# A decoder layer on one core: TensorE's order in the first row tile of a group of heads, with the packed halves apart, the reciprocals earlier and the values product in two halves

## The chip, the cores and the metric

The kernel runs on one core of a Trainium2 chip. The metric is the device time of the whole program in microseconds (us), the median of several runs; lower is better. Matrix products, transposes and weight loads run on TensorE (PE, weight loads shown as PEld), elementwise work on VectorE (DVE), exponentials and copies on ScalarE (ACT), small elementwise work on GpSimd (POOL); DMAs are issued from SyncE (SP). Each engine works through its own instructions in the order in which they are written, and the engines wait for one another only through semaphores.

## What is computed

One layer of a decoder: causal-by-multiplication attention with 16 heads, a second attention in which the layer's own rows are mixed by a softmax over a context, and a gated feed-forward part whose weights are packed in four bits.

```python
def reference(x, ctx_1024, Wq, Wk, Wv, Wo, xWq, xbq, xWk, xbk, gate_p, gate_s, up_p, up_s, down_p, down_s):
    # x: (4, 512, 512), 16 heads of 32
    x = x + attn(layernorm(x));  x = x + xattn(layernorm(x), ctx_1024);  return x + ffn(layernorm(x))

def attn(x):
    q, k, v = (x @ Wq), (x @ Wk), (x @ Wv)             # each reshaped to (B, T, 16, 32)
    scores = einsum('bthd,bshd->bhts', q, k) * tril(ones((T, T)))
    out = einsum('bhts,bshd->bthd', softmax(scores / T ** 0.5), v)
    return out.reshape(B, T, 512) @ Wo
```

The mask multiplies the scores: beyond the diagonal a score is 0, not minus infinity, so those columns still carry a weight, exp(0 - max), in the sum and in the product with the values.

## The kernel before

**Tiling.** The four batches (n = 0 to 3) go one after the other. A batch's attention is cut into 16 units (`UNITS`): four groups of four heads (`HG`), and in each group four row tiles of 128 rows (`TT`), u = 4 * group + row tile. Row tile i looks at (i + 1) * 128 columns (`wide`), so the first row tile of a group (u = 0, 4, 8, 12) is the narrowest and the fourth the widest. What lies beyond is one sum of values (`v_beyond`), scaled by one exponential (`e_zero`).

**The steps of one head j of one unit u**, each on its engine:

- `scores` (L929, PE) multiplies queries and keys of head j into bank j, once the exponentials of that head one unit back have read it;
- `row_max` (L1600, DVE) scales, masks and takes the largest of each row; `shift` (L763, POOL) negates it;
- `exp` (L1257, ACT) writes the weights `prob`;
- `turn` (L940, PE) transposes them, one 128x128 block at a time, into one of the banks 4, 5 and 7;
- `turned` (L1273 on ACT for heads 0 to 2, or 0 and 1 in a fourth row tile; L1610 on DVE for the rest) copies the transposed weights out, `prob_t`.

And once per unit: `recips` (L970, PE) turns the four columns of reciprocals into one bank of the same three, `recip_out` (L1279, ACT) copies it out; `values` (L961, PE) multiplies the transposed weights with V, four heads beside one another in columns of 32 (a 128x32 tile of the array), and `divide` (L1638, DVE) scales the product. Per 128 columns `values` has four matmuls, one per head, and for row tiles 0 to 2 four more for what lies beyond. All of them are float32, and a float32 matmul into a 128x32 tile is two records in the trace.

**Repacking.** Once per group a piece of the packed feed-forward weights is transposed as well: `repack` (L1036, PE) writes twelve 16-bit transposes, six into each of two banks; the first half is cast out by ACT (`pk_t`, L1293), the second by DVE (L1651), and SP stores both.

**The three shared banks.** Turns, reciprocals and the two packed halves go through banks 4, 5 and 7 in turn. A step's place in that sequence is its slot; `turn_slot`, `recip_slot` and `pack_slot` give it, and the bank is slot modulo three. Before PE writes slot s it waits (`turn_read`) until slot s - 3 has been read, by whichever engine reads that one.

**The order on PE** is written out by hand in `body` (L1201 on). In unit u, for each head j: the scores of unit u + 1, then the turn of unit u. After head 3 come the reciprocals and the values of unit u - 1. In the first row tile of a group (u = 4, 8, 12) both packed halves of the group before stand behind head 1. ACT's, DVE's and POOL's orders are written out in the same way; ACT's place for the cast of the first packed half is behind the copy of the turned head 1 (L1500).

In the text below, S(u,j) is a scores instruction, T(u,j) a turn, R(u) the reciprocals and V(u) the values of unit u.

Of the kernel before, what the change touches and what calls it, by code (L numbers as in the profile page):

```python
# [36 lines left out]
F16 = mybir.dt.float16  # L37
# [9 lines left out]
P = 128  # L47
# [5 lines left out]
TT = T // P  # L53
KT = D // P
HG = HEADS // 4
UNITS = HG * TT
# [35 lines left out]
def decoder_layer(nc, x, ctx_1024, Wq, Wk, Wv, Wo, xWq, xbq, xWk, xbk, gate_p, gate_s, up_p, up_s, down_p, down_s, out):  # L92
    with ExitStack() as ctx:
        def sem(name):
            return ctx.enter_context(nc.semaphore(name))
# [28 lines left out]
        def sb(name, shape, dt):  # L124
            return first.enter_context(nc.sbuf_tensor(name, shape, dt))
# [20 lines left out]
        pk_16 = sb("pk_16", [P, 6, C], F16)  # L146
# [9 lines left out]
        ident16 = sb("ident16", [P, P], F16)  # L156
# [98 lines left out]
        pt_act, pt_dve, av_done, o_done, o_hi, o_lo = (sem(n) for n in ("pt_act", "pt_dve", "av_done", "o_done", "o_hi", "o_lo"))  # L255
# [5 lines left out]
        pk_conv, pk_full, pk_out0, pk_out1, pk_stored = (sem(n) for n in ("pk_conv", "pk_full", "pk_out0", "pk_out1", "pk_stored"))  # L261
# [14 lines left out]
        ROWS = 4 * UNITS  # L276
        wide = [(i + 1) * P for i in range(TT)]

        def turn_slot(h):


            return h + 2 * (max(0, h - 2) // 16) + max(0, h // 4 - 1)

        def copied_by_act(u):

            return 2 if u % TT == TT - 1 and u < UNITS - 1 else 3

        def act_copies(n, u):

            return sum(copied_by_act(v) for v in range(UNITS)) * n + sum(copied_by_act(v) for v in range(u + 1))  # L290

        def vector_copies(n, u):

            return 4 * (n * UNITS + u + 1) - act_copies(n, u)

        def pack_slot(r, half):
            return (turn_slot(16 * r + 17) + 1 if r < HG - 1 else recip_slot(UNITS - 2) + 1) + half

        def recip_slot(u):
            return turn_slot(4 * u + 7) + 1 if u < UNITS - 1 else pack_slot(HG - 1, 1) + 1  # L300

        def turn_bank(slot):
            return bank[(4, 5, 7)[slot % 3]]

        def turn_read(n, slot):

            for u in range(UNITS):
                if slot == recip_slot(u):
                    return rden_out, n * UNITS + u + 1
                for j in range(4):  # L310
                    if slot == turn_slot(4 * u + j):
                        mine = copied_by_act(u)
                        return (pt_act, act_copies(n, u) - mine + j + 1) if j < mine else (pt_dve, vector_copies(n, u) - 3 + j)
            r, half = next((r, half) for r in range(HG) for half in range(2) if slot == pack_slot(r, half))
            return (pk_out0, pk_out1)[half], n * (NB // B) + r + 1
# [10 lines left out]
        def beyond_units(n, u):  # L326

            return n * HG * (TT - 1) + u // TT * (TT - 1) + min(u % TT + 1, TT - 1)
# [544 lines left out]
        def _(pe):  # L873
# [58 lines left out]
            def turn(n, u, j):  # L932
                i, slot = u % TT, turn_slot(4 * u + j)
                pe.wait_ge(exp_done, n * ROWS + 4 * u + j + 1)
                if slot < 3:
                    pe.wait_ge(att_lo, n * KT + (2, 3, 4)[slot])
                if slot >= 3:
                    pe.wait_ge(*turn_read(n, slot - 3))
                for k in range(wide[i] // P):
                    mm = pe.transpose(turn_bank(slot)[:, P * k:P * k + P], prob[:, u % 2, j, P * k:P * k + P], ident[:])  # L940
                mm.then_inc(t_full, 1)

            def values(n, u):

                hg, i = u // TT, u % TT
                pe.wait_ge(pt_act, act_copies(n, u))
                pe.wait_ge(pt_dve, vector_copies(n, u))
                if u == 0:
                    pe.wait_ge(v_out, n * TT + TT)
                if u >= 1:  # L950
                    pe.wait_ge(o_done, n * UNITS + u)
                blocks = wide[i] // P
                at = P * (u % 2)
                if i < TT - 1:
                    pe.wait_ge(v_zero_done, beyond_units(n, u))
                for k in range(blocks + (i < TT - 1)):
                    for j in range(4):
                        h = 4 * hg + j
                        lhs, rhs = (V[:, k, DH * h:DH * h + DH], prob_t[:, u % 2, j, P * k:P * k + P]) if k < blocks else \
                                   (v_zero[:, u % 2, DH * j:DH * j + DH], ident[:])  # L960
                        mm = pe.matmul(bank[6][32 * j:32 * j + 32, at:at + P], lhs, rhs, start=(k == 0), stop=(k == blocks - (i == TT - 1)))  # L961
                mm.then_inc(av_done, 1)

            def recips(n, u):

# [56 lines left out]
                        mm = pe.transpose(bank[CONTEXT_BANK[k]][:, P * m:P * m + P], e_p[:, m, P * k:P * k + P], ident[:])  # L1022
                    mm.then_inc(att_full, 1)

            def repack(n, r):
                nb = n * (NB // B) + r
                pe.wait_ge(pk_conv, 6 * nb + 6)
                for half in range(2):
                    pe.wait_ge(*turn_read(n, pack_slot(r, half) - 3))
                    bk = turn_bank(pack_slot(r, half))[:].bitcast(F16)  # L1030

                    tiles = [[(0, 0), (1, 0)], [(0, 1), (1, 1)], [(2, 0), (3, 0)]] if half == 0 else \
                            [[(2, 1), (3, 1)], [(4, 0), (4, 1)], [(5, 0), (5, 1)]]
                    for q in range(3):
                        for e, (a, w) in enumerate(tiles[q]):
                            mm = pe.transpose(bk[:, 256 * q + P * e:256 * q + P * e + P], pk_16[:, a, P * w:P * w + P], ident16[:])  # L1036
                    mm.then_inc(pk_full, 1)

            def product(m, x, which, pair, slot, nb):

# [160 lines left out]
            def body(n, last):  # L1201
                for u in range(UNITS):
                    for j in range(4):
                        if u + 1 < UNITS:
                            scores(n, u + 1, j)
                        turn(n, u, j)
                        if j == 3 and u == UNITS - 1 and not last:
                            pe.wait_ge(ln_done[0], (n + 2) * TT)
                            spread(0, n + 1, 0)
                        if j == 1 and u == UNITS - 1:  # L1210
                            values(n, u - 1)
                        if j == 3 and u > 0:
                            recips(n, u - 1)
                            if u < UNITS - 1:
                                values(n, u - 1)
                        if j == 1 and u % TT == 0 and u > 0:
                            repack(n, u // TT - 1)
                repack(n, HG - 1)
                recips(n, UNITS - 1)
                values(n, UNITS - 1)  # L1220
                between(n, True, not last)

            walk(body)(pe)


# [814 lines left out]
```

## Time and profile before

| | |
|---|---|
| median of 3 runs | 1477.64 us (1476.62 to 1477.94) |
| the profiled execution | 1479.39 us, of which its span 1477.7 us |
| busy share of the span | PE 96%, DVE 67%, ACT 48%, POOL 26% |
| granted TensorE clock | 1.00 |
| attention stages | about 70 to 135, 201 to 264, 333 to 396 and 467 to 528 us |
| one group of heads inside them | 15.13 us |

The page gives busy time per engine over the span, in 40 slices; the attention stages are those in which PE falls to 8 or 9 tenths while ACT rises. The timeline lists instructions in order of start; in it the number in brackets is the idle time of that engine ahead of the instruction, with what ended it.

### The profile page before, as it was taken

What the parts mean: (1) busy time and instruction counts of PE and PEld (TensorE: products, weight loads), DVE (VectorE), ACT (ScalarE), POOL (GpSimd) and SP (SyncE); (2) the same over time, 40 slices, a digit from 0 to 9 for tenths busy, and PEclk for the clock granted to TensorE, in tenths of its full rate; (3) what the DMA queues carried; (4) which work ended last, traced back from release to release, by engine and by line L of the source; (5) the groups of instructions that cost most, each with busy time, mean ns of one, the idle gap of its engine ahead of it and who ended that gap; (6) DMA issues with size and microseconds to landing.
All of it is one profiled execution on the core that took longest, in us unless ns stands there. A gap on an engine that the chain in (4) does not pass through costs nothing.

```text
span 1477.7 us, 26838 instructions
## 1 busy us (share of the span) xinstructions
PE 1422.8 (96%) x8896; PEld 718.8 (49%) x8896; DVE 990.5 (67%) x2125; ACT 716.6 (48%) x1660; POOL 380.5 (26%) x691
## 2 busy tenths in 40 slices
PE   6989998998998999999999999999999999999999
PEld 3465456556645654344444444444444444444444
DVE  7786688678668767886566666665665766665533
ACT  5795279239716845344354353353343443533532
POOL 0053225304373436521221112112112212212100
PEclk9999999999999999999999999999999999999999
DMA  7554622352456521000000001001001001000011
GB/s 249 143 159 125 171 70 83 113 161 66 142 160 171 180 63 45 17 24 25 31 14 22 17 17 33 17 17 35 17 17 32 17 16 33 17 17 1 0 58 57
DMA packets 76877, 98.01 MB, mean 66 GB/s; under 512 B 8000, under 2 KB 60736, under 8 KB 76224
## 3 DMA queue, kind: packets, MB, share of 16 engines
q1 hardware_dynamic: 76736, 96.23, 21.5%
q8 instruction: 76, 1.25, 0.4%
q14 instruction: 65, 0.53, 0.1%
HBM read 68.94 MB, written 27.26 MB: 65 GB/s over the span
## 4 chain that ended last, share of the span: by engine, by line
PE 84%; issue 5%; ACT 5%; DVE 4%; POOL 1%; DMA 0%; ACTq 0%; POOLq 0%; DVEq 0%; SPq 0%
PE bank L876 25%; PE bank L877 24%; PE bank L878 24%; ACT prob L1257 3%; PE bank L940 3%; PE bank L961 2%; PE bank L929 1%; PE bank L889 1%; PE bank L1001 1%; PE bank L1016 1%; PE bank L970 1%; PE bank L1011 1%; ACT prob_t L1273 1%; DVE xt L1585 1%; PE bank L1022 1%
## 5 line engine op out<-in xcount | busy, mean ns | idle before, releaser
L876 PE MATMUL bank<-xs,G 128*128 128x512 f16 x896 | 339.8, 379 | 2.5 <-issue 1.4
L877 PE MATMUL bank<-xs,G 128*128 128x512 f16 x896 | 339.6, 379 | 0.0
L878 PE MATMUL bank<-xs,G 128*128 128x512 f16 x896 | 339.6, 379 | 0.0
L1345 ACT COPY c<-bank 128x512 f32<-128x512 f32 x192 | 111.4, 580 | 220.2 <-PE bank L878 215.4
L1730 DVE TENSOR_TENSOR c<-bank,c 128x512 f32<-128x512 f32 x128 | 88.1, 689 | 193.7 <-PE bank L878 193.7
L876 PE MATMUL bank<-Wd,hid 128*128 128x512 f16 x512 | 194.1, 379 | 2.8 <-DVE X L1784 2.8
L878 PE MATMUL bank<-Wd,hid 128*128 128x512 f16 x512 | 194.0, 379 | 0.0
L877 PE MATMUL bank<-Wd,hid 128*128 128x512 f16 x512 | 194.0, 379 | 0.0
L748 POOL TENSOR_TENSOR c<-c,m 128x512 f32<-128x512 f32 x64 | 82.4, 1287 | 389.2 <-ACT c L1345 389.2
L1784 DVE SCALAR_TENSOR_TENSOR X<-bank,col,X 128x512 f32<-128x512 f32 x128 | 95.4, 750 | 101.5 <-PE bank L878 101.3
L1600 DVE CUSTOM_DVE_ANT_0 bank<-bank,mask,col 128x128 f32<-128x128 f32 (+3 forms) x256 | 139.3, 549 | 25.8 <-issue 17.2
L1257 ACT ACTIVATE prob<-bank,nmx 128x128 f32<-128x128 f32 (+3 forms) x256 | 146.6, 581 | 0.7
L876 PEld LDWEIGHTS bank<-xs,G 128*128 128x128 f16 x896 | 87.7, 98 | 114.2 <-ACT c L1345 6.1
L878 PEld LDWEIGHTS bank<-xs,G 128*128 128x128 f16 x896 | 87.7, 98 | 105.7
L877 PEld LDWEIGHTS bank<-xs,G 128*128 128x128 f16 x896 | 87.7, 98 | 103.1
L940 PE MATMUL bank<-ident,prob 128*128 128x128 f32 x640 | 111.9, 277 | 13.0 <-ACT prob L1257 3.8
L1368 ACT CAST hid<-c 128x512 f16<-128x512 f32 x128 | 79.2, 619 | 90.4 <-DVE c L1744 87.2
L1360 ACT ACTIVATE c<-c,col 128x512 f32<-128x512 f32 x96 | 69.4, 723 | 94.1 <-DVE c L1730 94.1
L763 POOL TENSOR_TENSOR nmx<-zero,mx 128x1 f32<-128x1 f32 x256 | 51.2, 200 | 236.1 <-DVE mx L1600 207.4
L1750 DVE TENSOR_TENSOR hid<-c,hid 128x512 f16<-128x512 f32 x128 | 86.1, 713 | 25.7 <-ACT hid L1368 25.7
L705 POOL TENSOR_TENSOR w_sum<-w_full 128x384 f32<-128x384 f32 (+1 forms) x30 | 22.1, 737 | 314.2 <-DVE w_full L1711 314.1
L940 PEld LDWEIGHTS bank<-ident,prob 128*128 128x128 f32 x640 | 76.0, 140 | 30.8 <-issue 19.3
(192 smaller groups left out, 2406.0 us busy)
## 6 DMA issues: line engine op xcount, KB each, us to landing
stack<-qk_dram SPq DMA_DIRECT2D x128, 128.0 KB, 3.3
sc_in<-scale_t SPq DMA_DIRECT2D x30, 384.0 KB
qk_dram<-qk SPq DMA_DIRECT2D x32, 256.0 KB, 2.8
packed_t<-pk_t SPq DMA_DIRECT2D x32, 192.0 KB, 2.0
pk_in<-packed_t SPq DMA_DIRECT2D x30, 192.0 KB
X<-in_x_dram SPq DMA_DIRECT2D x4, 1024.0 KB, 6.2
pk_in<-L_ffn_gate_W_packed_dram SPq DMA_DIRECT2D x16, 256.0 KB, 2.7
pk_in<-n_L_ffn_up_W_packed_dram SPq DMA_DIRECT2D x16, 256.0 KB, 3.1
```

Of the source, the lines that this page charges most:

```text
L748: nc.gpsimd.tensor_tensor(c22[x][:], c22[x][:], m5[x][:], ALU.add).then_inc(c22_out, 1)
L876: pe.matmul(o, lhs(0), rhs(0), start=first, stop=False, skip_group_check=onto)
L877: pe.matmul(o, lhs(0), rhs(1), start=False, stop=False, skip_group_check=onto)
L878: return pe.matmul(o, lhs(1), rhs(0), start=False, stop=stop, skip_group_check=onto)
L940: mm = pe.transpose(turn_bank(slot)[:, P * k:P * k + P], prob[:, u % 2, j, P * k:P * k + P], ident[:])
L1257: nc.scalar.activation(prob[:, u % 2, j, 0:wide[i]], bank[j][:, 0:wide[i]], ACT.Exp, bias=nmx[:, u % 2, j:j + 1], accum_out=den[:, u % 2, ...
L1345: nc.scalar.copy(dst[:], bank[BANK_Y if which == M5 else x][:]).then_inc(c_copied, 1)
L1368: nc.scalar.copy(hid[:, beta, q, r, 0, :], quarter(1, idx)[:]).then_inc(hid_hi, 1)
L1600: nc.vector.tensor_tensor_reduce(out=bank[j][:, 0:wide[i]], in0=bank[j][:, 0:wide[i]], in1=mask[:, P * (3 - i):P * (3 - i) + wide[i]], sca ...
L1730: nc.vector.tensor_tensor(dst[:], bank[at][:], dst[:], ALU.add).then_inc(comb, 1)
L1750: nc.vector.tensor_tensor(hid[:, beta, q, r, 1, :], quarter(1, idx)[:], hid[:, beta, q, r, 0, :], ALU.subtract).then_inc(hid_lo, 1)
L1784: nc.vector.scalar_tensor_tensor(xv, bank[4 + t][:], C_OUT, xv, ALU.mult, ALU.add).then_inc(acc_out, 1)
```

## The change

Only the order on PE in units 4, 8 and 12 of each batch is different, twelve places in all, and the slots with it. ACT, DVE, POOL and SP execute the same instructions in the same order as before; only the bank numbers of some of their copies are others.

- The first packed half goes behind head 0's turn, the second behind head 1's, instead of both behind head 1's.
- The reciprocals of unit u - 1 go behind the second packed half, instead of behind head 3.
- The values of unit u - 1 (always a fourth row tile, 16 matmuls) are cut in two: eight behind head 2's turn, eight behind head 3's.

```diff
+        slots_in_turn = []
+        for u in range(UNITS):
+            for j in range(4):
+                slots_in_turn.append(("turn", 4 * u + j))
+                if u > 0 and u % TT == 0 and j < 2:
+                    slots_in_turn.append(("pack", u // TT - 1, j))
+                if u > 0 and j == (1 if u % TT == 0 else 3):
+                    slots_in_turn.append(("recip", u - 1))
+        slots_in_turn += [("pack", HG - 1, 0), ("pack", HG - 1, 1), ("recip", UNITS - 1)]
+
         def turn_slot(h):
-            return h + 2 * (max(0, h - 2) // 16) + max(0, h // 4 - 1)
+            return slots_in_turn.index(("turn", h))
...
         def pack_slot(r, half):
-            return (turn_slot(16 * r + 17) + 1 if r < HG - 1 else recip_slot(UNITS - 2) + 1) + half
+            return slots_in_turn.index(("pack", r, half))
         def recip_slot(u):
-            return turn_slot(4 * u + 7) + 1 if u < UNITS - 1 else pack_slot(HG - 1, 1) + 1
+            return slots_in_turn.index(("recip", u))
...
-            def values(n, u):
+            def values(n, u, parts=(0, 1)):
                 hg, i = u // TT, u % TT
+                total = wide[i] // P + (i < TT - 1)
+                ks = range(0 if 0 in parts else total // 2, total if 1 in parts else total // 2)
...
-                for k in range(blocks + (i < TT - 1)):
+                for k in ks:
...
-                mm.then_inc(av_done, 1)
+                if 1 in parts:
+                    mm.then_inc(av_done, 1)
...
-            def repack(n, r):
+            def repack(n, r, half):
...
-                        if j == 3 and u > 0:
+                        first_tile = u % TT == 0 and u > 0
+                        if first_tile and j < 2:
+                            repack(n, u // TT - 1, j)
+                        if u > 0 and j == (1 if first_tile else 3):
                             recips(n, u - 1)
-                            if u < UNITS - 1:
-                                values(n, u - 1)
-                        if j == 1 and u % TT == 0 and u > 0:
-                            repack(n, u // TT - 1)
-                repack(n, HG - 1)
+                        if first_tile and j > 1:
+                            values(n, u - 1, (j - 2,))
+                        if j == 3 and 0 < u < UNITS - 1 and not first_tile:
+                            values(n, u - 1)
+                repack(n, HG - 1, 0)
+                repack(n, HG - 1, 1)
                 recips(n, UNITS - 1)
                 values(n, UNITS - 1)
```

PE's order in unit 4 of the first batch, before, from the turn of head 0 to the first scores of unit 6 (`prob` is a turn, `stack` scores, `pk_16` a packed half, `r_col` the reciprocals, `prob_t,V` the values):

```order
L940 MATMUL bank5<-ident,prob 128x128
L929 MATMUL bank1<-stack 128x256
L940 MATMUL bank7<-ident,prob 128x128
L1036 MATMUL bank4<-ident16,pk_16 128x128 x6
L1036 MATMUL bank5<-ident16,pk_16 128x128 x6
L929 MATMUL bank2<-stack 128x256
L940 MATMUL bank7<-ident,prob 128x128
L929 MATMUL bank3<-stack 128x256
L940 MATMUL bank4<-ident,prob 128x128
L970 MATMUL bank5<-ident,r_col 32x128 x4
L961 MATMUL bank6<-prob_t,V 32x128 x16
L929 MATMUL bank0<-stack 128x384
```

The same stretch of PE's order in the changed kernel, from the first packed half on:

```order
L1047 MATMUL bank7<-ident16,pk_16 128x128 x6
L938 MATMUL bank1<-stack 128x256
L949 MATMUL bank4<-ident,prob 128x128
L1047 MATMUL bank5<-ident16,pk_16 128x128 x6
L982 MATMUL bank7<-ident,r_col 32x128 x4
L938 MATMUL bank2<-stack 128x256
L949 MATMUL bank4<-ident,prob 128x128
L972 MATMUL bank6<-prob_t,V 32x128 x8
L938 MATMUL bank3<-stack 128x256
L949 MATMUL bank5<-ident,prob 128x128
L972 MATMUL bank6<-prob_t,V 32x128 x8
L938 MATMUL bank0<-stack 128x384
```

The reciprocals now stand ahead of the scores and turns of heads 2 and 3 and go into bank 7, which the first packed half wrote; before, it was the turn of head 3 that followed the first packed half in its bank. With their waits, PE's rows of the reciprocals and of head 3's turn at this place, before:

```order
L940 MATMUL bank4<-ident,prob 128x128 [waits pk_out0,exp_done]
L970 MATMUL bank5<-ident,r_col 32x128 [waits rcol_done,pk_out1]
```

and in the changed kernel, in its order:

```order
L982 MATMUL bank7<-ident,r_col 32x128 [waits rcol_done,pk_out0]
L949 MATMUL bank5<-ident,prob 128x128 [waits pk_out1,exp_done]
```

The wait for `pk_out0`, ACT's cast of the first packed half, moved from the turn of head 3 to the reciprocals, and that for `pk_out1`, DVE's cast, the other way. ACT's order around that cast, the same before and after but for line and bank numbers:

```order
L1273 COPY prob_t<-bank5 128x128 [waits av_done,t_full]
L1257 ACTIVATE prob,den<-bank3,nmx 128x128 [waits t_full,shift_done]
L1266 ACTIVATE e_zero<-nmx 128x4 [waits shift_done,v_zero_done,den_done]
L1273 COPY prob_t<-bank7 128x128 [waits av_done,t_full]
L1293 CAST pk_t<-bank4 128x768 [waits sd_stored,pk_full]
L1257 ACTIVATE prob,den<-bank0,nmx 128x256 [waits t_full,shift_done]
L1273 COPY prob_t<-bank7 128x128 [waits av_done,t_full]
```

The cast stays behind the copy of T(4,1); nothing moved here.

## Rows read from the trace of the kernel before

**Rows 1.** The page: PE's granted clock, engines' busy time and PE's largest chain shares.

```profile
PE 1422.8 (96%) x8896; PEld 718.8 (49%) x8896; DVE 990.5 (67%) x2125; ACT 716.6 (48%) x1660; POOL 380.5 (26%) x691
...
PEclk9999999999999999999999999999999999999999
```

**Rows 2.** Windows, two whole groups of batch 1: us, busy per engine, clock, DMA share.

```profile
218.24:233.38 15.14, 13.61 (x209) 9.88 (x205) 12.84 (x51) 14.20 (x53) 7.51 (x26) 1.00 0.23 76
233.38:248.51 15.13, 13.61 (x208) 9.87 (x204) 12.55 (x50) 14.19 (x53) 7.31 (x26) 1.00 0.27 86
```

**Rows 3.** ACT's timeline, unit 8's place in batch 1: start, duration, line, idle before.

```profile
230.19 0.27 ACT L1273 COPY prob_t<-bank 128x128 f32<-128x128 f32 x1 [0.54 <-PE bank L940]
...
230.81 0.26 ACT L1273 COPY prob_t<-bank 128x128 f32<-128x128 f32 x1
230.95 0.82 ACT L1293 CAST pk_t<-bank 128x768 int16<-128x768 f16 x1
231.64 0.51 ACT L1257 ACTIVATE prob<-bank,nmx 128x256 f32<-128x256 f32 x1
...
232.10 0.29 ACT L1273 COPY prob_t<-bank 128x128 f32<-128x128 f32 x1
...
233.01 0.49 ACT L1257 ACTIVATE prob<-bank,nmx 128x256 f32<-128x256 f32 x1
...
233.97 0.37 ACT L1273 COPY prob_t<-bank 128x256 f32<-128x256 f32 x1 [0.38 <-PE bank L940]
```

**Rows 4.** PE's timeline at the same place, from T(8,0) to T(9,0).

```profile
229.77 0.28 PE L929 MATMUL bank<-stack 128*128 128x256 f16 x1
229.89 0.27 PE L940 MATMUL bank<-ident,prob 128*128 128x128 f32 x1
230.00 0.27 PE L929 MATMUL bank<-stack 128*128 128x256 f16 x1
230.10 0.27 PE L940 MATMUL bank<-ident,prob 128*128 128x128 f32 x1
230.21 0.83 PE L1036 MATMUL bank<-ident,pk 128*128 128x128 f16 x12
230.88 0.27 PE L929 MATMUL bank<-stack 128*128 128x256 f16 x1
231.22 0.30 PE L940 MATMUL bank<-ident,prob 128*128 128x128 f32 x1
231.35 0.27 PE L929 MATMUL bank<-stack 128*128 128x256 f16 x1
231.92 0.30 PE L940 MATMUL bank<-ident,prob 128*128 128x128 f32 x1 [0.29 <-ACT pk_t L1293]
232.15 0.42 PE L970 MATMUL bank<-ident,r_col 128*32 128x128 f32 x8
232.39 1.06 PE L961 MATMUL bank<-prob_t,V 128*32 128x128 f32 x32
233.38 0.34 PE L929 MATMUL bank<-stack 128*128 128x384 f16 x1
233.55 0.38 PE L940 MATMUL bank<-ident,prob 128*128 128x128 f32 x2
```

**Rows 5.** All waits of the span, longest first: waited for us, times, longest us.

```profile
PE bank L940 <- ACT pk_t L1293: 3.5, 12, 0.3
```

**Rows 6.** PE's timeline: sixteen value records, then scores; reciprocals, then a packed half.

```profile
235.59 0.40 PE L961 MATMUL bank<-prob_t,V 128*32 128x128 f32 x8
235.81 0.40 PE L961 MATMUL bank<-ident,v_zero 128*32 128x128 f32 x8
236.14 0.39 PE L929 MATMUL bank<-stack 128*128 128x512 f16 x1
...
261.25 0.43 PE L970 MATMUL bank<-ident,r_col 128*32 128x128 f32 x8
261.61 0.84 PE L1036 MATMUL bank<-ident,pk 128*128 128x128 f16 x12
```

**Rows 7.** DVE's timeline at the place: the row maximum behind the first scores of unit 10.

```profile
233.90 0.63 DVE L1600 CUSTOM_DVE_ANT_0 bank<-bank,mask,col 128x384 f32<-128x384 f32 x1 [0.71 <-issue]
```

**Rows 8.** PE's timeline: its longest idle in the second half's start.

```profile
560.64 0.39 PE L876 MATMUL bank<-att_t,o_t 128*128 128x512 f16 x1 [1.19 <-DVE o_t L1585]
```

**Rows 9.** Windows, a stretch that holds the wait of rows 8.

```profile
535.00:590.00 55.00, 53.45 (x263) 26.07 (x262) 40.29 (x87) 25.81 (x43) 26.50 (x22) 1.00 0.14 41
```

More of the change, by code:

```diff
@@ L953, in values @@
                 at = P * (u % 2)
-                if i < TT - 1:
+                if i < TT - 1 and 1 in parts:
                     pe.wait_ge(v_zero_done, beyond_units(n, u))
-                for k in range(blocks + (i < TT - 1)):
+                for k in ks:
                     for j in range(4):
@@ L1023, in context_out @@
                     mm.then_inc(att_full, 1)
-            def repack(n, r):
+            def repack(n, r, half):
                 nb = n * (NB // B) + r
                 pe.wait_ge(pk_conv, 6 * nb + 6)
[L1028 to L1037, printed above, removed]
+                pe.wait_ge(*turn_read(n, pack_slot(r, half) - 3))
+                bk = turn_bank(pack_slot(r, half))[:].bitcast(F16)
+                tiles = [[(0, 0), (1, 0)], [(0, 1), (1, 1)], [(2, 0), (3, 0)]] if half == 0 else \
+                        [[(2, 1), (3, 1)], [(4, 0), (4, 1)], [(5, 0), (5, 1)]]
+                for q in range(3):
+                    for e, (a, w) in enumerate(tiles[q]):
+                        mm = pe.transpose(bk[:, 256 * q + P * e:256 * q + P * e + P], pk_16[:, a, P * w:P * w + P], ident16[:])
+                mm.then_inc(pk_full, 1)
             def product(m, x, which, pair, slot, nb):
```

## The prediction, made before the changed kernel ran

> **What bounds the kernel now.** The page comes first: TensorE (PE) is busy nearly all the time at full granted clock, the other engines far less [rows 1]. That is an average over stages. The change touches only attention, so the next view is the windows of two whole groups of heads [rows 2]. There PE is busy 13.6 of 15.13 us, and ScalarE (ACT) 14.2. ACT is the fuller engine: 15.13 - 14.19 leaves it 0.94 us of idle time in a group. ACT's timeline shows where that is: 0.54 us ahead of the copy of T(8,0) at 230.19 and 0.38 us ahead of the copy of T(9,0) at 233.97 [rows 3], together 0.92 us, which is all of it. Both times ACT waits for a turn on PE. So everywhere else in a group ACT runs without a pause and sets the pace, and at the first row tile PE does. A group becomes shorter or longer by as much as these two turns come earlier or later, and a delay of T(9,0) isn't made good afterwards, because ACT has no pause left to give until the next such place.
>
> The first gap lies ahead of everything that the change moves: T(8,0) follows V(6), and both keep their places. The second one is the change's: T(9,0) stands behind T(8,3), R(7), V(7) and S(10,0). PE's timeline of the place [rows 4] is to be read as a chain. T(8,3) starts at 231.92, released by ACT's cast of the first packed half (230.95 + 0.82 = 231.77, and 0.15 us until PE is at work). From there PE runs without a pause: R(7) at 232.15, V(7) at 232.39, S(10,0) at 233.38, T(9,0) at 233.55, and ACT's copy starts 0.42 us later. The same wait for the cast stands 12 times in the list of waits, with the same 0.3 us [rows 5]: three places in each of four batches, all alike.
>
> **What the change does to that chain.** The cast itself can't come sooner. ACT does it right behind the copy of T(8,1), at 230.95, and reaches that copy at 230.81 after other work [rows 3]. In the new order T(8,1) stands behind the first packed half. The twelve packed transposes take 230.88 - 230.21 = 0.67 us, one half 0.335 us, so T(8,1) moves from 230.10 to 230.44. A turn's copy follows its start by 0.30 us (229.89 to 230.19), so it is ready at 230.74, still 0.07 us before ACT comes. The second half then waits for the copy of T(8,0) and ends at about 230.95; DVE's cast of it moves by some 0.05 us, which nothing waits for. So the cast on ACT still ends at 231.77.
>
> What waits for that cast is different. The reciprocals now take the bank of the first packed half. PE executes in order, so behind R(7) stand S(9,2), T(8,2), S(9,3) and T(8,3); the first three ran before 231.92 in the old order, beside the cast [rows 4]. PE idles from 230.95 to 231.92, and all of this comes after it.
>
> The pieces, each from a row:
> - R(7) and then a full-array instruction: 261.61 - 261.25 = 0.36 us [rows 6].
> - scores, then a turn: 229.89 - 229.77 = 0.12 us [rows 4].
> - a turn, then 128x32 work: 232.15 - 231.92 = 0.23 us [rows 4].
> - sixteen value records, then scores: 236.14 - 235.59 = 0.55 us [rows 6]. That is half of V(7), which has 32 records and takes 0.99 us in one piece (233.38 - 232.39).
>
> New chain from 231.92: R(7) 0.36, S(9,2) 0.12, T(8,2) 0.23, first half of V(7) 0.55, S(9,3) 0.12, T(8,3) 0.23, second half 0.55, sum 2.16 us. S(10,0) starts at 234.08. Before it started at 233.38, 1.46 us behind the wait. The place becomes 0.70 us longer.
>
> The 0.70 us have two sources. Three instructions at 0.11 to 0.12 us that used to run beside the cast now run behind it: 0.34 us. And PE changes more often between the full array and 128x32 tiles. A turn is followed by its neighbour after 0.11 us (230.10 to 230.21) but by 128x32 work after 0.23, and 32 value records at the 0.0275 us that eight of them take (235.81 - 235.59 = 0.22) make 0.88 of the 0.99 us. Each change costs about 0.12 us. Before there are two behind the wait, afterwards five: 3 x 0.12 = 0.36 us. The split as such isn't visible in the trace of before; bounded by rows, a change costs between nothing (if it hid beside the wait for a semaphore) and 0.13 us. I take 0.12, since all four kinds of neighbours in the rows show 0.11 to 0.13.
>
> The Trainium skill, "TensorEngine Tiling (Array Packing)", section "Key Properties", says that changing the tiling mode drains TensorE, and "TensorE: Matmul & The Clock Gate", section "Step-by-step: what each phase is for", puts a drain at about 128 cycles, by my estimate 0.05 us at 2.4 GHz. By that the place would be 0.34 + 3 x 0.05 = 0.5 us longer and the kernel 6 us; the rows show more than twice that per change, and the sum goes by them.
>
> **Does ACT hide some of it?** T(8,2) moves from 231.22 to 231.92 + 0.36 + 0.12 = 232.40, and its copy to 232.70 instead of 232.10 [rows 3]. The 1.49 us of ACT's work between that copy and the idle time (233.97 - 0.38 - 232.10) end at 234.19. T(9,0) starts at 234.08 + 0.17 = 234.25, and its copy at 234.67. So PE stays last, ACT idles 0.48 us in place of 0.38, and ACT's copy moves by the whole 0.70 us. ACT copies R(7) out ahead of the exponential that started at 233.01 [rows 3], so even 0.6 us later its bank is free before T(9,0). DVE's row maximum for S(10,0) starts 0.52 us behind it, as before [rows 7], so it moves along. POOL sits idle between its small steps.
>
> **The sum.** 12 places x 0.70 us = 8.4 us on the chain. Between attention stages PE is the engine that is always at work, and its products follow the end of attention, so nothing there absorbs it. On the profiled execution (1479.39 us, of which 1477.7 are span) this gives 1487.8; profiled executions lie 1.75 us above the median here, so the median goes from 1477.64 to 1486.0 us.
>
> **Rivals.**
> - *The changes of tile shape cost little, ACT limits the place.* If a change were free, T(8,2) would start at 231.92 + 0.24 + 0.11 = 232.27 and be copied at 232.57; 1.49 us later ACT is at 234.06, 0.09 us behind the 233.97 of before. PE would have T(9,0) at about 233.63, its copy at 234.05. 12 x 0.09 = 1.1 us: 1478.7, within measurement. For it: the rows show each change with a long burst on one side, not around single turns. Against it: all of them show it. 8%. Part of it (0.3 to 0.55 us a place, 1481 to 1484.3, the 0.05 us drain included): 17%.
> - *Faster.* The idle time ahead of R(7) is the only new wait. If the bank were free when the second packed half ends (230.95), the same 2.16 us would bring S(10,0) to 233.11, 0.27 us sooner, and ACT's second gap would shrink: 12 x 0.27 = 3.2 us, 1474.4. Each 0.1 us that the cast ended earlier would bring 0.1 us; the place breaks even only when it ends 0.70 us sooner, at 231.07. ACT would have to start it at 230.25 or before, and its order puts it behind the copy of T(8,1), which PE now delivers later. 4%.
> - *Slower still.* T(8,1)'s copy has 0.07 us to spare. If the packed half costs more in front of it, the cast and all behind it slip as well: with 0.1 to 0.2 us, 12 x that = 1.2 to 2.4 us on top, 1487.2 to 1488.4. A fall of the clock during the 1 us idle would cost more; a pause of 1.19 us [rows 8] lies in a stretch with a granted clock of 1.00 [rows 9], so I give it almost nothing. 6% together.
> - *The change doesn't act*: both orders differ in all 12 places, so this has no share of its own.
>
> **How the numbers follow.** The forecast, 0.60 to 0.80 us a place, has 65% and 1484.8 to 1487.2; its centre is 1486.0. The range reaches down over the partly hidden changes and up over the late turn: 1480.5 to 1489. It leaves out the first rival and the gain. A measurement tells about 0.2% (3.0 us) from no change: slower by more is the forecast, the partial case and the last rival, 0.88; same is the first rival, 0.08; faster 0.04.
>
> **What would show it.** In the new profile the list of waits should have the reciprocals (PE) waiting for ACT's `pk_t` 12 times with nearly 1 us each, and no turn waiting for it. The group should take 15.8 us in place of 15.13, with ACT's busy time in it unchanged at 14.2. PE's timeline should show S(10,0) 2.1 to 2.2 us behind the start of R(7), with the two halves of V(7) 0.55 us each up to the next scores. ACT should idle some 0.5 us twice, before the copies of T(8,2) and T(9,0). If the group takes 15.2 us, the changes of tile shape were free; if R(7) starts before 231.6 by this clock, the bank wait was misjudged; if the group is right and the total isn't, something behind attention gave time back.

## The result and the profile after

| | before | after |
|---|---|---|
| median of 7 runs | 1477.64 us | 1483.59 us |
| lowest and highest | 1476.62 to 1480.85 us | 1482.52 to 1485.41 us |
| the profiled execution, and its span | 1479.39 us, 1477.7 us | 1483.77 us, 1482.0 us |
| ratio after to before | | 1.0037, 95% interval 1.0028 to 1.0046 |

The change makes the kernel 5.5 to 6 us slower. The forecast was 8.4 us slower, 1486.0 us, with a range of 1480.5 to 1489. The measured median lies in that range, but below the band that the prediction called its forecast proper, 1484.8 to 1487.2.

The list of waits of the changed kernel answers [rows 5] (engine, line, what it waited for, us in total, times, longest):

```profile
ACT prob_t L1288 <- PE bank L949: 18.6, 40, 0.6
PEld bank L982 <- ACT pk_t L1308: 10.8, 12, 0.9
PE bank L982 <- ACT pk_t L1308: 8.7, 12, 0.7
```

No turn waits for the cast any more. The reciprocals (L982) do, 12 times, each time 0.73 us for the matmul and 0.90 us for its weight load, where the turn had waited 0.29 us [rows 4]. ACT waits for turns 40 times for 18.6 us, against 28 times and 15.2 us before: twelve waits more.

PE's timeline of the same place, T(8,0) to T(9,0) in batch 1, answers [rows 4]:

```profile
233.11 0.28 PE L938 MATMUL bank<-stack 128*128 128x256 f16 x1
233.23 0.27 PE L949 MATMUL bank<-ident,prob 128*128 128x128 f32 x1
233.34 0.50 PE L1047 MATMUL bank<-ident,pk 128*128 128x128 f16 x6
233.67 0.27 PE L938 MATMUL bank<-stack 128*128 128x256 f16 x1
233.78 0.27 PE L949 MATMUL bank<-ident,prob 128*128 128x128 f32 x1
233.94 0.49 PE L1047 MATMUL bank<-ident,pk 128*128 128x128 f16 x6
235.17 0.42 PE L982 MATMUL bank<-ident,r_col 128*32 128x128 f32 x8 [0.73 <-ACT pk_t L1308]
235.52 0.28 PE L938 MATMUL bank<-stack 128*128 128x256 f16 x1
235.64 0.27 PE L949 MATMUL bank<-ident,prob 128*128 128x128 f32 x1
235.85 0.65 PE L972 MATMUL bank<-prob_t,V 128*32 128x128 f32 x16
236.42 0.28 PE L938 MATMUL bank<-stack 128*128 128x256 f16 x1
236.54 0.27 PE L949 MATMUL bank<-ident,prob 128*128 128x128 f32 x1
236.75 0.64 PE L972 MATMUL bank<-prob_t,V 128*32 128x128 f32 x16
237.32 0.34 PE L938 MATMUL bank<-stack 128*128 128x384 f16 x1
237.50 0.38 PE L949 MATMUL bank<-ident,prob 128*128 128x128 f32 x2
```

I call the time from the first scores of the unit (233.11) to the first 384-wide scores (237.32) the length of the place: 4.21 us here, 3.61 us in [rows 4] (229.77 to 233.38). PE stands idle behind the second packed half, the reciprocals start at 2.06 us into the place, and the rest follows in 2.15 us without a pause.

ACT's timeline there, with both of the pauses that the new order gives it:

```profile
234.29 0.82 ACT L1308 CAST pk_t<-bank 128x768 int16<-128x768 f16 x1
...
235.95 0.27 ACT L1288 COPY prob_t<-bank 128x128 f32<-128x128 f32 x1 [0.37 <-PE bank L949]
...
237.91 0.37 ACT L1288 COPY prob_t<-bank 128x256 f32<-128x256 f32 x1 [0.50 <-PE bank L949]
```

The cast starts 1.18 us into the place, as in [rows 3]. The windows of the two groups, which answer [rows 2], are longer by the same 0.60 us:

```profile
217.37:233.11 15.74, 13.85 (x209) 9.69 (x205) 13.04 (x51) 14.31 (x52) 7.53 (x26) 1.00 0.21 69
233.11:248.84 15.73, 13.84 (x208) 9.68 (x205) 12.75 (x50) 14.30 (x52) 7.34 (x26) 1.00 0.24 76
```

**Where the time went.** All twelve places take 4.21 or 4.22 us: 12 x 0.60 = 7.2 us. Yet the spans of the two traces differ by 4.3 us and the medians by 5.95. I laid the starts of PE's instructions in both traces beside one another. The first attention stage starts 0.9 us later in the changed kernel's trace, before any instruction that the change moves. The distance then grows by 1.8 us in each of the first three attention stages, 0.60 us a place. In the fourth stage it falls by 0.3 us, and in the feed-forward part it shrinks again.

The 0.9 us at the start stand in the windows from 22 to 30 us, where both kernels do the same work, in the order before and after (columns as in [rows 2]):

```profile
22.00:30.00 8.00, 7.02 (x34) 2.93 (x35) 6.73 (x10) 7.57 (x14) 0.00 (x0) 1.00 0.56 194
```

```profile
22.00:30.00 8.00, 7.00 (x26) 2.92 (x27) 6.70 (x10) 6.66 (x12) 0.00 (x0) 0.79 0.54 188
```

The granted clock was 1.00 there in one trace and 0.79 in the other. Of all fourteen traces seven have the one value and seven the other. The kernel before has 1.00 in two traces and 0.79 in a third, whose program differs from it only in a later load, so this difference doesn't come from the change.

What the kernel before loses in the fourth stage and behind it stands in its own trace, which paused where the changed kernel doesn't:

```profile
480.32 0.73 PE L961 MATMUL bank<-prob_t,V 128*32 128x128 f32 x17 [2.09 <-issue]
...
1019.68 0.39 PE L876 MATMUL bank<-xs,G 128*128 128x512 f16 x1 [1.20 <-issue]
```

"issue" is time in which the engine waited for nothing that the profile shows. The first group of the last batch (units 0 to 3, from the first scores of unit 1 to those of unit 5) takes 15.80 us in that trace instead of the 13.31 us of the other three batches. The expectations below call it the second group. Two questions are open at this point: whether the 0.60 us has the two sources that the prediction named, and what these pauses are.

### The profile page after: what moved, and what is told of

Same layout as the page of the kernel before. It is cut to its first block, busy times and chain, and to the rows that moved or that the text cites. A ratio compares the mean times of both kernels' runs of the same rounds, so it can differ in the third digit from the quotient of the medians.

```text
span 1482.0 us, 26866 instructions
## 1 busy us (share of the span) xinstructions
PE 1427.4 (96%) x8896; PEld 717.7 (48%) x8896; DVE 992.5 (67%) x2125; ACT 718.5 (48%) x1660; POOL 380.8 (26%) x691
## 4 chain that ended last, share of the span: by engine, by line
PE 85%; ACT 5%; issue 4%; DVE 4%; POOL 1%; DMA 0%; ACTq 0%; POOLq 0%; DVEq 0%; SPq 0%
PE bank L885 24%; PE bank L886 24%; PE bank L887 24%; PE bank L949 3%; ACT prob L1272 3%; PE bank L972 2%; PE bank L938 1%; PE bank L982 1%; PE bank L898 1%; PE bank L1013 1%; PE bank L1028 1%; PE bank L1023 1%; ACT pk_t L1308 1%; DVE xt L1600 1%; ACT prob_t L1288 1%
## 5 line engine op out<-in xcount | busy, mean ns | idle before, releaser
L1288 ACT COPY prob_t<-bank 128x128 f32<-128x128 f32 (+3 forms) x180 | 81.5, 453 | 18.6 <-PE bank L949 18.6
```

Source lines behind the costliest of these rows:

```text
L1288: nc.scalar.copy(prob_t[:, u % 2, j, 0:wide[i]], turn_bank(turn_slot(4 * u + j))[:, 0:wide[i]]).then_inc(pt_act, 1)
```

## The experiments

Each was timed against runs of the kernel before on the same chip, but not all on one chip: the kernel before has medians of 1477.95, 1477.99 and 1478.47 us on the three, and ratios and differences below are to its own chip's. "Place" is the length defined above. It is the same within 0.01 us in nearly all twelve places of a kernel; a few single places are 0.02 to 0.06 us longer, and one near 482 us can be longer by more, which the text then says.

### The kernel before once more

No edit.

> The kernel before, unchanged, once more with a trace. The trace at hand has two pauses of PE that no semaphore explains, 2.09 us at 480.3 in the fourth batch and 1.20 us at 1019.7; the trace of the changed kernel has neither. Theory A, that they belong to this kernel's instruction stream: both stand there again at the same places, and each of the twelve places takes 3.61 us again from the first scores to the first scores two units on. Theory B, that they are chance: the pauses are gone or elsewhere, and the span is then 1474 to 1476 us. The time against itself should be 1.000 within 0.1%.

Ratio 1.0001 (0.9992 to 1.001). Places 3.61 us (one, behind the first pause, 4.03), and both pauses are there again, 1.56 us at 479.83 and 0.89 us at 1019.88. The first group of the last batch takes 16.13 us. So theory A holds in two traces of two. This group is longer than in the first trace although the pause is shorter; the granted clock fell behind it (columns as in [rows 2]):

```profile
474.00:478.00 4.00, 3.52 (x53) 2.55 (x46) 3.65 (x16) 4.00 (x14) 1.74 (x8) 1.00 1.01 289
479.83:483.00 3.17, 3.17 (x35) 2.53 (x36) 0.69 (x3) 0.67 (x5) 0.11 (x1) 0.50 0.89 325
```

### The changed kernel with whole values

```diff
-                        if first_tile and j > 1:
-                            values(n, u - 1, (j - 2,))
-                        if j == 3 and 0 < u < UNITS - 1 and not first_tile:
+                        if j == 3 and 0 < u < UNITS - 1:
                             values(n, u - 1)
```

> The changed kernel with one part undone: the values product is whole again, behind head 3's turn. Packed halves apart and reciprocals early as in the change. Theory (waits and tile-shape changes add up): two changes between full array and 128x32 tiles fewer than in the changed kernel, so a place takes 3.96 us (3.61 before, 4.21 changed), 12 x 0.35 = 4.2 us above the kernel before in the attention stages. Rival (the wait of the reciprocals alone does it, cutting is free): 4.2 us a place as in the changed kernel, 7.2 us in all.

The place takes 3.97 us. PE's timeline at the place, from the reciprocals on:

```profile
233.49 0.43 PE L982 MATMUL bank<-ident,r_col 128*32 128x128 f32 x8 [0.73 <-ACT pk_t L1306]
233.85 0.28 PE L938 MATMUL bank<-stack 128*128 128x256 f16 x1
233.97 0.27 PE L949 MATMUL bank<-ident,prob 128*128 128x128 f32 x1
234.08 0.27 PE L938 MATMUL bank<-stack 128*128 128x256 f16 x1
234.19 0.27 PE L949 MATMUL bank<-ident,prob 128*128 128x128 f32 x1
234.39 1.08 PE L972 MATMUL bank<-prob_t,V 128*32 128x128 f32 x32
235.40 0.34 PE L938 MATMUL bank<-stack 128*128 128x384 f16 x1
```

With the same work and the same wait, two changes of tile shape fewer, one into 128x32 and one back, save 4.21 - 3.97 = 0.24 us, on average 0.12 us each. Cutting the values product isn't free, and the rival falls. The whole kernel, at 1484.39 us (1.0042, 1.0028 to 1.0056), isn't faster than the changed one, and the places don't explain it. Its trace has a pause of 2.66 us at 1021.5 that the changed kernel's trace hasn't, and a granted clock of 0.61 and 0.71 in the 5 us behind it (see below).

### The reciprocals in the other bank

```diff
-                if u > 0 and j == (1 if u % TT == 0 else 3):
+                if u > 0 and j == (2 if u % TT == 0 else 3):
                     slots_in_turn.append(("recip", u - 1))
```

Only the slots change: the execution order is that of the changed kernel.

> The changed kernel's order on every engine, but the reciprocals and head 2's turn exchange their banks: the reciprocals wait for ACT's copy of head 1's turn, and head 2's turn waits for ACT's cast of the packed half. Theory (the cast holds up whatever stands behind it on PE): the reciprocals start 1.4 us into the place instead of 2.06, head 2's turn at 2.15, and the place takes 3.83 us, 12 x 0.22 = 2.6 us above the kernel before. Rival (the cost is only in the five changes of tile shape, which stay): 4.2 us a place, 7 us in all.

The place takes 3.86 us (one of the twelve, in a stretch of granted clock 0.50 behind a pause of 2.17 us at 482.5, 4.70). PE's timeline:

```profile
232.32 0.42 PE L982 MATMUL bank<-ident,r_col 128*32 128x128 f32 x8
232.68 0.28 PE L938 MATMUL bank<-stack 128*128 128x256 f16 x1
233.11 0.30 PE L949 MATMUL bank<-ident,prob 128*128 128x128 f32 x1 [0.15 <-ACT pk_t L1308]
233.34 0.65 PE L972 MATMUL bank<-prob_t,V 128*32 128x128 f32 x16
```

The reciprocals start 1.36 us into the place (230.96), and what waits for the cast is head 2's turn, for 0.15 us. The reciprocals with the change of shape behind them (0.36 us) and head 2's scores (0.12 us) now run beside the cast, and the turn starts 0.09 us later than the reciprocals had: 0.39 us expected, 0.35 measured. Which instruction gets the cast's bank decides it. What is left over the kernel before is 0.25 us. Behind the wait stand one pair of scores and turn more (0.22 us) and two changes of shape more (0.24), but the reciprocals no longer (0.24 from their start to that of the values in [rows 4]), which makes 0.22. Ratio 1.0009 (1.000 to 1.0018), 1.2 us by the medians: most of the loss is gone with a change of banks alone. The places alone would cost 12 x 0.25 = 3.0 us.

### Only the packed halves apart

From the kernel before, with recips and whole values behind head 3 and with the slots to match:

```diff
-                        if j == 1 and u % TT == 0 and u > 0:
-                            repack(n, u // TT - 1)
+                        if first_tile and j < 2:
+                            repack(n, u // TT - 1, j)
```

> From the kernel before, only the two packed halves are apart (first behind head 0's turn, second behind head 1's); reciprocals and whole values behind head 3. Theory: it is now head 2's turn that takes the first half's bank and waits for ACT's cast, at 2.15 us into the place, with head 3's scores and turn behind it: 3.84 us a place in place of 3.61, 2.8 us in all. Rival (the early first half lets ACT cast sooner): the cast starts before 1.18 us into the place and the place takes 3.61 us or less.

The place takes 3.83 us (one of twelve, in a stretch of granted clock 0.50 behind a pause, 4.50). Head 2's turn waits for the cast, 2.15 us into the place:

```profile
231.67 0.28 PE L938 MATMUL bank<-stack 128*128 128x256 f16 x1
...
233.82 0.30 PE L949 MATMUL bank<-ident,prob 128*128 128x128 f32 x1 [0.70 <-ACT pk_t L1306]
...
234.56 1.06 PE L972 MATMUL bank<-prob_t,V 128*32 128x128 f32 x32
```

The cast starts 1.19 us into the place, no sooner than before. So even the mildest part of the change costs 0.22 us a place. It hands the cast's bank to a turn that stands earlier on PE, and one pair of scores and turn, 2 x 0.11 us, now comes behind the wait; tile shapes change no more often than before. Total 1484.11 us (1.0039, 1.0024 to 1.0055; four executions), again more than the 2.6 us of the places; its trace pauses for 2.32 us at 483 and 2.92 us at 1024. That trace is of the slowest of the four executions, 1488.5 us.

### The changed kernel with late reciprocals

```diff
-                if u > 0 and j == (1 if u % TT == 0 else 3):
+                if u > 0 and j == 3:
                     slots_in_turn.append(("recip", u - 1))
...
-                        if u > 0 and j == (1 if first_tile else 3):
+                        if u > 0 and j == 3:
                             recips(n, u - 1)
```

> The changed kernel with another part undone: the reciprocals stand behind head 3's turn as in the kernel before; packed halves apart and values in two halves as in the change. Theory: head 2's turn waits for the cast (2.15 us into the place), then first half of the values, head 3's scores and turn, reciprocals, second half: 4.09 us a place, 5.8 us above the kernel before in the attention stages. Rival (the early reciprocals are the whole of the loss): 3.61 to 3.7 us a place.

4.08 us a place; 1481.94 us (1.0026, 1.0016 to 1.0035), with a pause of 1.62 us at 484 in its trace. That is the 0.22 us of the halves alone and two changes of tile shape more, 0.24 us. The early reciprocals are only 0.13 us of the 0.60.

### Values and reciprocals ahead of head 3's turn

From the kernel before; packed halves both behind head 1 as there. The calls and the slot behind head 3's turn are left out in these units, which the cut doesn't show.

```diff
                             scores(n, u + 1, j)
+                        first_tile = u % TT == 0 and u > 0
+                        if first_tile and j == 3:
+                            values(n, u - 1)
+                            recips(n, u - 1)
                         turn(n, u, j)
...
+                if first_tile and j == 3:
+                    slots_in_turn.append(("recip", u - 1))
                 slots_in_turn.append(("turn", 4 * u + j))
```

> From the kernel before, with both packed halves behind head 1 again, but in the first row tile the whole values product and then the reciprocals stand between head 3's scores and head 3's turn, so that they fill the wait for the cast. Only two changes of tile shape. Theory: values start 1.8 us into the place, reciprocals at 2.7, head 3's turn at 3.04, the next unit's first turn at 3.33 instead of 3.78, so ACT's second pause (0.38 us) closes; its copy of the reciprocals may come 0.1 us late. A place takes 3.2 to 3.35 us and 12 x 0.28 to 0.38 us are gained: 3.4 to 4.6 us below the kernel before, 1473 to 1474 us. Rival (ACT can't use the earlier turn, something else of its inputs comes last, such as the row maxima): within 1 us of the kernel before.

The place takes 3.18 us, 0.43 less than before. PE's timeline shows no wait for the cast at all:

```profile
229.51 0.27 PE L942 MATMUL bank<-stack 128*128 128x256 f16 x1
229.71 1.08 PE L976 MATMUL bank<-prob_t,V 128*32 128x128 f32 x32
230.61 0.40 PE L986 MATMUL bank<-ident,r_col 128*32 128x128 f32 x8
230.94 0.33 PE L953 MATMUL bank<-ident,prob 128*128 128x128 f32 x1
231.11 0.33 PE L942 MATMUL bank<-stack 128*128 128x384 f16 x1
```

The values product starts before the cast has ended (229.11 + 0.82 = 229.93) and needs nothing from it. The reciprocals have the cast's bank now, and they come 0.68 us behind its end. ACT's second pause of [rows 3] is gone: it reaches the copy of T(9,0) without waiting for PE. Twelve places give 5.2 us, but the kernel, at 1476.11 us, gained only 1.8 by the medians (0.9984, 0.9975 to 0.9993), less than the 3.4 to 4.6 us expected: its trace has a pause of 2.31 us at 476 and one of 2.60 us at 1014.

### The changed kernel once more

No edit.

> The changed kernel, unchanged, once more with a trace. Two traces of the kernel before each lose about 2.5 to 2.8 us in the second group of the last batch (a pause of PE with no semaphore behind it, 1.56 and 2.09 us) and 0.9 to 1.2 us at 1020; the one trace of the changed kernel loses nothing there. If that is tied to the instruction stream, both are missing again, and the places take 4.21 us again. If it is chance, a pause of 1.5 to 2.5 us shows up near 482 us. Time: 1.0037 to 1.0045 of the kernel before.

Places 4.21 us again, and no pause at either spot. 1483.64 us, 1.0041 (1.0027 to 1.0055).

### The large loads later, in the kernel before

```diff
                     load_half(3, 1, 1)
-                    load_first()
...
                         load_operand(0, B11, 0, 0)
                         load_sum(1)
+                        load_first()
```

> The kernel before, but SP issues the two large loads of the first weights (1.8 and 0.5 MB, which occupy the DMA engines from 469 to 484 us) only behind the first group of the last batch, near 485 us. Theory (PE runs out of instructions there because their fetch stands behind this traffic): the pause near 480 is gone, the last batch's second group takes 13.3 us instead of 15.8 to 16.1, and the time falls by up to 2.5 us, to about 1475.5, unless another fetch meets the load at its new place. Rival (the pause is tied to the place in the program): it stays at 480 and the time is unchanged.

The pause at 480 is gone; the last batch's first group takes 13.31 us, like the others. The windows from 466 to 484 us, in the order before and late load (columns as in [rows 2]):

```profile
466.00:484.00 18.00, 13.84 (x181) 9.55 (x183) 13.79 (x56) 14.79 (x58) 6.54 (x28) 1.00 0.83 229
```

```profile
466.00:484.00 18.00, 15.93 (x221) 11.39 (x220) 14.77 (x60) 16.35 (x63) 7.15 (x30) 1.00 0.45 133
```

With the DMA engines 0.83 busy PE gets through 13.84 us of work in 18, with 0.45 through 15.93. The instruction queues have a few packets in the same stretch. That would fit an instruction fetch that stands behind the loads, but it isn't shown: no view says which packet carried which instructions. What is shown is that the pause is gone when the loads move. Full DMA engines alone don't make it: in the last version below they are 0.98 to 1.00 busy from 482 to 491 us, and PE doesn't pause. The time fell by 1.1 us (0.9991, 0.9982 to 1.000, at the edge of the noise), less than the pause of one trace, so not every execution seems to pause that long. A pause of 0.92 us at 1017.6 stays.

### The late load with the values first

The two edits together.

> The order with values and reciprocals ahead of head 3's turn (3.18 us a place) together with the late load. Theory: the gain of 12 x 0.43 = 5.2 us stands in full once the pause at 476 (2.5 us in its trace) is gone: 1472 to 1473 us, 0.996 to 0.9975 of the kernel before. Rival (the pause moves with the load): 1475 to 1476 us as without it.

1474.26 us, 0.9976 (0.9966 to 0.9986), not the 1472 to 1473 expected. No pause near 476, but 2.37 us at 1011, so the gain, 3.7 us, is again less than the 5.2 us of the places.

### The late load in the changed kernel

> The changed kernel with the two large loads of the last batch behind its first group. Its own traces show no pause at 480 us, so nothing should be won there: 1483 to 1484 us. Against the kernel before with the same late load (1476.93) that would be about 6.5 us: 12 places x 0.60 = 7.2 us, less the 0.9 us pause at 1018 us that the changed kernel doesn't have. Rival (the late load helps here as it did there): 1482 us or less.

1483.66 us, the same as without it, as expected of a kernel that didn't pause there.

### The position in the instruction stream

```diff
+            for _ in range(28):
+                pe.sem_inc(passed, 1)
             pe.wait_ge(const_done, 3)
             pe.wait_ge(ld_s, 48)
```

> The kernel before with the late load, and 28 semaphore increments that nobody waits for at the start of PE's program, where PE waits for the first loads anyway; it then has as many instructions as the changed kernel (26866). Theory (the pause at the head of the loop's second round depends on where the loop lies in the instruction stream): in ten traces it is 0.9 to 1.2 us with 26838 instructions, 2.4 to 2.9 us with 26854, none with 26866, so it should be gone: 0.9 to 1.2 us less than the 1476.93 of the late load alone, about 1476. Rival (the pause hangs on what the attention part does): it stays, 1477 us.

The pause at the head of the loop's second round is gone. 1476.08 us, 0.9984 (0.9975 to 0.9993) of the kernel before, where the late load without the increments had 0.9991 on another chip. The difference of the ratios, 1.0 us, is about the pause of 0.92 us, but the intervals overlap, so the time alone doesn't prove it.

With 12 increments in the kernel that has the values first and the late load:

> Values and reciprocals ahead of head 3's turn, late load, and 12 such increments at the start of PE's program, so that it too has 26866 instructions. Theory: the pause of 2.37 us at 1011 us and the lower granted clock behind it (together 3.9 us in its trace without the increments) are gone: 1470 to 1471.5 us, 0.995 to 0.996 of the kernel before. Rival: the pause stays and the time is 1474.3 us as without.

No pause, and 1470.76 us: 0.9952 (0.9938 to 0.9966) of the kernel before, where it was 0.9976 without the increments, on another chip; both the medians and the ratios put 3.5 us between them. This is the fastest version.

The pause at this spot in all fourteen traces, by the number of instructions on the first line of the page:

| instructions | kernels | pause, us |
|---|---|---|
| 26838 | before, before again, before with late load | 1.20, 0.89, 0.92 |
| 26854 | whole values, halves alone, values first, values first with late load | 2.66, 2.92, 2.60, 2.37 |
| 26866 | changed (twice), changed with late load, other bank, late reciprocals, before padded, values first padded | none |

The traces show more than the number. With 26838 instructions PE pauses behind the ninth product of that round (`xs,G`, 128x512), in all three traces; with 26854 behind the first, in all four. That is eight products earlier, each with its weight load, so 16 instructions, and 16 is the difference of the two numbers. So the pause stays at one place in the sequence of instructions while the code slides past it.

## Why the prediction was right, and where it was off

**The bound was read rightly.** A turn that comes later at the second of ACT's two pauses lengthens the group by its full delay: every place is 0.60 us longer and a whole group too (15.73 against 15.13), and nothing inside attention made it good. The forecast of 15.8 us was 0.70 us a place.

**The wait moved as forecast.** The cast starts 1.18 us into the place in both kernels. The reciprocals and everything behind them come after it, and ACT idles 0.37 and 0.50 us before the two copies named.

**The chain behind the wait was right, its start 0.1 us too late.** The pieces were put at 2.16 us and measured 2.15 (0.35, 0.12, 0.21, 0.57, 0.12, 0.21, 0.57). But I let the reciprocals start where the turn had, 2.15 us into the place, and they started at 2.06. The reciprocals' first matmul follows the cast's end sooner than the turn's did. Of the 8.4 us forecast this is 1.1. Why it follows sooner isn't shown.

**Both sources are shown.** The halves alone move two instructions behind the wait and nothing else: 0.22 us, 0.11 each. The late reciprocals add two changes of tile shape: 0.25 us. Whole values take two away again: 0.24 us. So three instructions at 0.11 and three changes at 0.12, less the 0.09 us just named, are the 0.60. That the changes of shape cost this and not the number type or the cut alone is borne out by the rows around them: a float32 turn is followed by float32 values after 0.21 us and by other full-array work after 0.11.

By the Trainium skill's drain of about 128 cycles ("TensorE: Matmul & The Clock Gate", section "Step-by-step: what each phase is for") the prediction estimated 0.5 us for the place and 6 us for the kernel. The rows of before gave 0.70. Measured are 0.60 for the place and 0.12 us per change, so the rows had the size of that term and the start of the chain was the error. That the median moved by nearly 6 us doesn't bear the estimate out: the places cost 7.2.

**One step failed: "nothing there absorbs it".** The delay itself wasn't absorbed, but the kernel before lost time elsewhere that the changed one doesn't lose. The sum of the prediction ran from the median of before and took all its other time as fixed. With both pauses out of both kernels, on one chip (changed with late load, 1483.66; before with late load and increments, 1476.08), the difference is 7.6 us, near the 7.2 us of the places. On that chip the kernel before as it is has 1478.47 us. So it loses 2.4 us on average to what the late load and the increments take away, and of the 7.6 us only 5.2 are left; the first comparison measured 5.95, with an interval of about 4 to 7. The pauses stood in the trace of before, as idle time of PE with the releaser "issue"; the first group of the last batch, 15.80 us long, would have shown one of them.

**Part of the hit is luck.** A place of 0.60 us is the lower end of the forecast's 0.60 to 0.80. The total, 1483.59 us, fell out of its 1484.8 to 1487.2 and into the 1481 to 1484.3 of the rival in which the changes of shape are partly hidden. They are not hidden. The total lies there because of the pauses, which the prediction didn't have, and the range held because it was drawn wide for another reason.

**The rivals.** That tile-shape changes are free is refuted. The faster one, a free bank behind the second packed half, never came about in the changed kernel, but the other bank and above all the values-first order show that its mechanism was real: the idle time beside the cast can be used, by work that doesn't need the cast's bank.

## What to carry to other kernels

Where banks rotate and one reader is slow, look at which instruction gets the slow reader's bank: everything behind that instruction on the in-order engine pays for the wait. Put work there that needs neither the bank nor the reader, and put it ahead of the waiting instruction; cutting 128x32 work into pieces with full-array matmuls between them cost 0.24 us here for each further piece, one change out and one back. When an edit is worth a few us, compare the idle times without a releaser in both traces before believing the total: here 12 instructions that do nothing took about 3.5 us away. And compare the granted clock of stretches that the edit doesn't touch: it made 0.9 us between two traces.

## What the runs showed of the hardware

- A change from full-array to 128x32 float32 matmuls and back costs 0.24 us (4.21 against 3.97 us a place with one such pair fewer). The rows put 0.10 to 0.13 us on each direction.
- PE can pause with no semaphore to wait for. Near 480 us, beside 2.3 MB of loads, it paused 1.56 to 2.32 us in six of nine traces of kernels with the early load (not in the two of the changed kernel and the one with whole values), and in none of five with the late load.
- At the head of the second round of a loop PE paused 0, about 1 or about 2.6 us, by the length of the program (the table above), and at a fixed place in the sequence of instructions. What happens at that place wasn't shown.
- After some of these pauses the granted clock fell. It did in all four traces with the pause of 2.37 to 2.92 us at the loop's second round, and in none of the three with 0.89 to 1.20 us. Near 480 us it fell to 0.50 behind pauses of 1.56, 2.17 and 2.32 us and stayed at 1.00 behind 1.62, 2.09 and 2.31, so the length of the pause alone doesn't decide it. Windows of the kernel with only the halves apart, before and after its 2.92 us pause:

```profile
1010.00:1020.00 10.00, 10.00 (x48) 4.51 (x47) 6.75 (x11) 0.72 (x1) 0.00 (x0) 1.00 0.02 6
1024.30:1029.70 5.40, 5.40 (x13) 1.89 (x14) 2.74 (x4) 1.06 (x2) 1.73 (x4) 0.50 0.19 46
1030.20:1040.00 9.80, 9.80 (x47) 4.39 (x45) 2.45 (x4) 5.42 (x10) 1.28 (x1) 1.00 0.10 31
```

For 5.4 us the clock stands at 0.50, that is 1.2 GHz, and 13 matmuls run in the time in which 25 would at 2.4 GHz, where they follow one another every 0.216 us (5.40 / 0.216). So this pause cost 2.92 us and then about 2.6 us more. PE had been busy without a break in the 10 us up to 1020. Behind the shorter pause of 1.20 us in the trace of before, matmuls follow one another every 0.22 us at once.
